# Transformer block on one core: the context projected a batch ahead, self-attention's values ahead of its transposes, and cross-attention's V padded with zeros

## The reference

```python
h = layernorm(x, ln1_g, ln1_b)
x = attention(h, h, a1_Wq, a1_Wk, a1_Wv, a1_Wo, a1_bo) + x        # self
h = layernorm(x, ln2_g, ln2_b)
x = attention(h, context, a2_Wq, a2_Wk, a2_Wv, a2_Wo, a2_bo) + x  # cross
h = layernorm(x, ln3_g, ln3_b)
u, gate = split(h @ ff_Wp + ff_bp)
return (u * gelu(gate)) @ ff_Wo + ff_bo + x
```

## Time and profile before

| | |
|---|---|
| median of 3 runs | 1007.19 us (997.95 to 1015.29) |
| the profiled execution | 1004.74 us |
| span in its trace | 1002.9 us |
| mean granted clock of TensorE | 0.966 of full speed |
| PE busy in the span | 931.9 us (93%) |
| DVE | 768.2 us (77%) |
| ACT | 672.5 us (67%) |
| POOL | 388.3 us (39%) |

### The profile page before, as it was taken

How to read it: one execution, slowest core, us unless ns; L and a number is a source line. 1 busy time by engine, 2 the same in 40 slices (tenths; PEclk the granted TensorE clock), 3 DMA queues, 4 the chain that set the end, 5 groups by cost and what they waited for, 6 DMA issues and landing times.

```text
span 1002.9 us, 21207 instructions
## 1 busy us (share of the span) xinstructions
PE 931.9 (93%) x7252; PEld 864.4 (86%) x7252; DVE 768.2 (77%) x1658; ACT 672.5 (67%) x2009; POOL 388.3 (39%) x498
## 2 busy tenths in 40 slices
PE   7799998899999999999997899899899897899998
PEld 6687877798989899999987798898898896799998
DVE  5576678979888988888897887886787877566674
ACT  5556556878786877777787678776677777343333
POOL 1211445534443444434333545544545555201010
PEclk9799999999999999999999899997899998899999
DMA  7311101224111111111142134212212212100100
GB/s 222 97 50 42 37 22 36 56 47 103 25 47 23 49 34 33 34 38 44 23 106 49 45 73 104 56 28 54 55 29 54 52 33 80 37 33 32 33 23 22
DMA packets 85745, 51.67 MB, mean 52 GB/s; under 512 B 43272, under 2 KB 79112, under 8 KB 85640
## 3 DMA queue, kind: packets, MB, share of 16 engines
q1 hardware_dynamic: 85640, 50.32, 19.3%
HBM read 41.64 MB, written 8.65 MB: 50 GB/s over the span
## 4 chain that ended last, share of the span: by engine, by line
PE 70%; DVE 13%; ACT 9%; issue 4%; DMA 2%; POOL 1%; SPq 1%; DVEq 0%; POOLq 0%
PE bank L1444 10%; PE bank L1445 9%; PE bank L1446 9%; PE bank L1461 5%; PE bank L1704 5%; PE bank L1684 5%; PE bank L1733 4%; PE bank L1734 4%; ACT p L809 3%; PE bank L1752 3%; PE bank L1754 3%; PE bank L1753 3%; PE bank L1713 1%; PE bank L1566 1%; PE bank L1567 1%
## 5 line engine op out<-in xcount | busy, mean ns | idle before, releaser
L613 POOL TENSOR_TENSOR oT_scaled<-oT,rsumT 128x256 f32<-128x256 f32 x128 | 98.2, 767 | 318.6 <-DVE oT L1239 177.4
L809 ACT ACTIVATE p<-bank,negmax 128x256 f32<-128x256 f32 (+1 forms) x512 | 207.6, 427 | 18.5 <-DVE negmax L1202 12.5
L1444 PE MATMUL bank<-hT_hi,w_hi 128*128 128x256 f32 x640 | 190.2, 297 | 8.5 <-DVE qkT_lo L1271 2.9
L1445 PE MATMUL bank<-hT_lo,w_hi 128*128 128x256 f32 x640 | 180.4, 282 | 0.0
L1446 PE MATMUL bank<-hT_hi,w_lo 128*128 128x256 f32 x640 | 180.3, 282 | 0.0
L1444 PEld LDWEIGHTS bank<-hT_hi,w_hi 128*128 128x128 f32 x640 | 123.3, 193 | 13.1 <-issue 10.2
L1445 PEld LDWEIGHTS bank<-hT_lo,w_hi 128*128 128x128 f32 x640 | 122.8, 192 | 0.0
L1446 PEld LDWEIGHTS bank<-hT_hi,w_lo 128*128 128x128 f32 x640 | 122.4, 191 | 0.0
L1733 PE MATMUL bank<-pT_hi,v_hi_lo 128*128 128x256 f32 (+1 forms) x384 | 102.2, 294 | 14.8 <-DVE oT L1239 4.9
L819 ACT CAST pT_hi<-bank 128x512 fp32r<-128x512 f32 x128 | 68.9, 591 | 67.6 <-PE bank L1704 67.5
L809 ACT ACTIVATION_READ_ACCUMULATOR p<-bank,negmax 128x1 f32 x512 | 110.0, 215 | 0.0
(11 more groups left out here) (204 smaller groups left out, 2788.8 us busy)
## 6 DMA issues: line engine op xcount, KB each, us to landing
rsumT<-rsums_dram SPq DMA_DIRECT2D x256, 64.0 KB, 2.8
w_stage<-in_weights SPq DMA_DIRECT2D x47, 256.0 KB, 4.5
x_in<-x_dram SPq DMA_DIRECT2D x24, 256.0 KB, 3.6
x_dram<-x_out SPq DMA_DIRECT2D x16, 256.0 KB, 3.3
l_x<-in_x SPq DMA_DIRECT2D x4, 512.0 KB, 5.2
x_dram<-l_out SPq DMA_DIRECT2D x4, 512.0 KB, 2.8
rsums_dram<-rsum SPq DMA_DIRECT2D x128, 2.0 KB, 3.2
out_dram<-x_out SPq DMA_DIRECT2D x8, 256.0 KB, 2.1
```

What stands on the lines that cost most here:

```text
L613: nc.gpsimd.tensor_tensor(on[:, :].rearrange("p (t q) -> p t q", t=NT), of[:, G % DEEP, :].rearrange("p (t q) -> p t q", t=NT), rT[:, G % ...
L809: last = nc.scalar.activation(p[:, G % 2, e, t * cols:(t + 1) * cols], scores_at(G, e, t), ACT.Exp, bias=negmax[:, G % 2, t, e:e + 1], acc ...
L1444: nc.tensor.matmul(dst, lh, rh, start=(i == 0), stop=False)
L1445: nc.tensor.matmul(dst, lh, rl, start=False, stop=False)
```

## The change

Three parts, in two kinds of step.

*The context a batch ahead.* A second pair of buffers holds cT_hi and cT_lo (`c_hi(b)`, `c_lo(b)`, by the parity of b; the room is taken from a buffer that served as filler). Transposes, rounding and low half of a cross batch's context move from steps i=3 and 4 of the batch before it to the last step (i=7) of the batch before that, and into bank 3. `project_keys(b+1, 0)` stays at i=4 and takes over the wait for `h_full`. DVE's `prepare_lo` of a cross batch moves from i=3 to i=4.

*One order.* In a self step `weighted_values(G-1)` now follows `scores(G+1)` at once, as in a cross step; ACT's `copy_low_values(G-1)` and DVE's `add_low_values(G-1)` move up ahead of `round_pT` and `pT_low` in theirs.

*Cross-attention's V.* V is laid out as head, 64 zeros, head for each pair, high halves in one plane and low halves in another. Six matmuls of 256 columns, where there were four, gather a pair's outputs in one half of a bank: high by high and high by low of the probabilities, and low by high, for each of the two heads. Nothing is copied or added: DVE's `normalise_o(G-2)` multiplies the bank by rT into `oT`, and POOL's `split_o` has two operations, two steps behind. POOL sets V's zeros, and those of the keys that DVE set before.

```diff
+            ch2 = sb("cT_hi2", [128, KT, SC], F32R, where=l1)
+            cl2 = sb("cT_lo2", [128, SC], F32R, where=l1)
@@ banks
-            return bank[4 if b == B else 7]
+            return bank[4 if b == B else 3]
@@ POOL step
+                if b == B - 1 and i == 4:
+                    zero_keys(0, G)
+                if b == B and i == 0:
+                    zero_keys(1, G)
+                if b == B - 1 and i == 5:
+                    zero_values(0, G - 1)
+                if b == B and i == 1:
+                    zero_values(1, G - 1)
...
-                if G >= 1:
+                if 1 <= G <= STEPS // 2:
                     split_o(G - 1)
+                if G >= STEPS // 2 + 2:
+                    split_o(G - 2)
@@ ACT step_self
+                if G >= 1:
+                    copy_low_values(G - 1)
                 round_pT(G)
                 softmax_pair(G + 1)
...
-                if G >= 1:
-                    copy_low_values(G - 1)
+                if turn and i == 7:
+                    round_context(B + 1)
@@ ACT step_cross
-                if i == 4 and more:
-                    round_context(b + 1)
...
-                copy_low_values(G - 1)
+                if G == STEPS // 2:
+                    copy_low_values(G - 1)
...
+                if i == 7 and b + 2 < 2 * B:
+                    round_context(b + 2)
@@ DVE
+            def normalise_o(G):
+                dve.wait_ge(y["o"], G + 1)
+                dve.wait_ge(*spread_until(G))
+                dve.wait_ge(y["o_norm" if G - DEEP < STEPS // 2 else "o_lo"], G - DEEP + 1)
+                nc.vector.tensor_tensor(of[:, G % DEEP, :].rearrange("p (t q) -> p t q", t=NT),
+                                        o_bank(G).rearrange("p (t q) -> p t q", t=NT),
+                                        rT[:, G % DEEP, :].rearrange("p (q t) -> p t q", t=NT),
+                                        ALU.mult).then_inc(y["o_sum"], 1)
@@ DVE step_self
+                if G >= 1:
+                    add_low_values(G - 1)
                 pT_low(G)
...
-                if turn and i == 4:
-                    zero_keys(0, G)
-                if G >= 1:
-                    add_low_values(G - 1)
@@ DVE step_cross
-                if i == 4 and more:
-                    context_low(b + 1)
...
-                add_low_values(G - 1)
+                if G == STEPS // 2:
+                    add_low_values(G - 1)
+                if G >= STEPS // 2 + 2:
+                    normalise_o(G - 2)
                 pT_low(G)
...
-                if i == 3:
+                if i == 4:
                     prepare_lo(b + 1)
...
+                if i == 7 and b + 2 < 2 * B:
+                    context_low(b + 2)
@@ PE
             def context(b):
                 pe.wait_ge(y["c_in"], 32 * (b - B + 1))
+                if b > B:
+                    pe.wait_ge(y["qk_lo"], query_product(b - 1, 1))
@@ PE weighted_values
+                if b >= B:
...
+                    for e in range(2):
+                        vc = slice(g * 3 * DH + e * DH, g * 3 * DH + e * DH + 128)
...
@@ PE step_self
                 scores(G + 1)
+                if G >= 1:
+                    weighted_values(G - 1)
                 transpose_p(G)
...
-                if G >= 1:
-                    weighted_values(G - 1)
@@ PE step_cross
-                if i == 3 and more:
+                if i == 4 and more:
                     pe.wait_ge(y["h_full"], KT * (b + 2))
-                    context(b + 1)
-                if i == 4 and more:
                     project_keys(b + 1, 0)
+                if i == 7 and b + 2 < 2 * B:
+                    context(b + 2)
```

More of the change, by code:

```diff
@@ L344, in v_src, with padded @@
             return v_bank(b, c)[0:v_rows(b), :].rearrange("p (g e d) -> p g e d", g=4, e=2)
+        def padded(c):
+            return vv[0:SC, :, 0:PAIRS * 3 * DH].rearrange("p j (g s d) -> p j g s d", g=PAIRS, s=3)[:, :, 4 * c:4 * c + 4, :, :]
         def v_dst(b, c, low):
+            if b >= B:
+                return padded(c)[:, int(low), :, 0:3:2, :]
             part = vv[0:v_rows(b), c // 2, c % 2 * 4 * 2 * VW:(c % 2 + 1) * 4 * 2 * VW]
@@ L391, in o_bank @@
         def o_bank(G):
-            return bank[6 if G < STEPS // 2 or G % 2 else 2]
+            return bank[6] if G < STEPS // 2 else bank[6 if G % 2 else 2][:, 0:S]
         def pT_both(G):
@@ L619, in split_o, with zero_values @@
+                nc.gpsimd.tensor_tensor(oh[:, G % PAIRS, :], full, ones[:, :], ALU.mult).then_inc(y["o_hi"], 1)
                 pool.wait_ge(y["o_hi"], G + 1)
-                nc.gpsimd.tensor_tensor(ol[:, G % PAIRS, :], on[:, :], oh[:, G % PAIRS, :].bitcast(F32),
+                nc.gpsimd.tensor_tensor(ol[:, G % PAIRS, :], full, oh[:, G % PAIRS, :].bitcast(F32),
                                         ALU.subtract).then_inc(y["o_lo"], 1)
+            def zero_values(c, read):
+                pool.wait_ge(y["o"], read)
+                pool.wait_ge(y["o_lo"], read - 1)
+                nc.gpsimd.memset(padded(c)[:, :, :, 1, :].bitcast(F32), 0.0).then_inc(v_zeros_ready, 1)
+                pool.wait_ge(v_zeros_ready, c + 1)
@@ new lines, in zero_keys @@
+            def zero_keys(c, read):
+                pool.wait_ge(y["scores"], read)
+                pool.wait_ge(y["o_lo"], read - 1)
+                for n, k_ in enumerate((kdh, kdl)):
+                    nc.gpsimd.memset(k_[0:DH, 4 * c:4 * c + 4, SC:2 * SC].bitcast(F32), 0.0).then_inc(zeros_step, 1)
+                    pool.wait_ge(zeros_step, 4 * c + 2 * n + 1)
+                    nc.gpsimd.memset(k_[DH:128, 4 * c:4 * c + 4, 0:SC].bitcast(F32), 0.0).then_inc(zeros_step, 1)
+                    pool.wait_ge(zeros_step, 4 * c + 2 * n + 2)
+                pool.sem_inc(zeros_ready, 1)
@@ L800, in round_context @@
                 act.wait_ge(y["cT"], b - B + 1)
[L801 removed]
+                nc.scalar.copy(c_hi(b)[:, :, :], c_src(b)).then_inc(y["cT_hi"], 1)
             def softmax_pair(G):
@@ L1320, in step_self @@
                     weights_lo(dve, 10 + i)
-                if turn and i == 4:
-                    zero_keys(0, G)
-                if G >= 1:
-                    add_low_values(G - 1)
+                if turn and i == 7:
+                    context_low(B + 1)
             def step_cross(G):
@@ L1388, in feed_forward @@
                         f_low(it, j - 1)
+                    if it == 0 and j == 0:
+                        normalise_o(STEPS - 2)
                     if it == 0 and j == 1:
-                        add_low_values(STEPS - 1)
                         weights_lo(dve, 25)
+                    if it == 0 and j == 2:
+                        normalise_o(STEPS - 1)
                     if it == 0 and j == 3:
@@ L1803, in project_values @@
                 else:
-                    last = context_product(dst, w, (ch[:, 0, :], cl[:, :], ch[:, 1, :]), False)
+                    last = context_product(dst, w, (c_hi(b)[:, 0, :], c_lo(b)[:, :], c_hi(b)[:, 1, :]), False)
                 last.then_inc(y["v"], 1)
             def project_keys(b, c):
-                pe.wait_ge(y["cT_lo"], b - B + 1)
+                pe.wait_ge(y["cT_lo"], b - B + (2 if c == 1 and b + 1 < 2 * B else 1))
                 if c == 1 or b == B:
@@ L1868, in step_self @@
                     project_out(b, 0, 3)
+                if turn and i == 7:
+                    context(B + 1)
             def step_cross(G):
```

54 lines of the change are left out of this document (31 added, 23 removed).

## The result

| | before | after |
|---|---|---|
| median of 20 runs each, us | 1008.77 | 1018.02 |
| span of the profiled execution | 1002.9 | 1012.3 |
| matmuls of PE | 7252 | 7380 |

The ratio is 1.0104, with a 95% interval of 1.0083 to 1.0125: the change costs one per cent. That is a small sum of large terms of both signs. The two spans differ by 9.4 us. Cut at the starts of the scores, they differ by +28.0 us in the self stage with the turn (380.7 to 408.7), −18.3 from there to the first scores of the last cross batch (268.9 to 250.6), −0.6 behind those (193.2 to 192.6) and +0.2 ahead of all.

A forecast was written before the change was run, and what follows sets the result against it. PE was taken to bound the self stage, with cross-attention looser, mostly at i=4 and 5. 1004.7 + 15.4 − 27 − 3 − 2 + 19 + 13 = 1020.1, forecast 1020 us; 8 in 10: 994 to 1041.

The forecast's parts named there:

- padded V: Cross-attention: 128 more weighted_values matmuls at 0.12 us each, with nothing on PE to cover them, +15.4 us.
- context ahead: Cross steps i=4 and 5: the 12.7 us wait and three quarters of the slow matmuls go, −27 us.
- wait for V: Self step i=5: PE idles 2.35 us for V's low half in each of eight batches, +19 us.
- clock's echo: Self batches: clock falls after that wait, 1.6 us a batch as middle of two rows, +13, bounds 0 and 26.
- turn: Between self and cross stages: POOL zeroes keys instead of DVE, shortening PE's waits, −3 us, bounds 0 and −4.25.
- end: Kernel's end: a shorter chain cuts PE's 4.4 us of waits for oT_lo, −2 us, bounds 0 and −4.4.
- The estimate of 1033: Whole kernel: time if the skill page's clock cycling puts the echo nearer its upper end, 1033 us.
- I take 0, bounds 0 and −4: Cross stage: relief of DVE, ACT and POOL by padded V gains 0, since neither DVE nor ACT sets the end.
- the self stage keeps its clock: Rival, self stage: the wait is there but no clock fall follows, 1007 us; chance 0.18.
- the context stays on the path: Rival, cross stage: wait moves to another operand, only 10 of the 27 us come back, 1037 us; chance 0.06.
- DVE's wait for the spread sums: Rival, cross steps: normalise_o waits for the rT transfer, late in the odd case only; +21, 1041 us; chance 0.08.
- the sign that I gave: Cross stage: no wait of DVE for rT of over a microsecond.

The follow-up runs named there:

- context alone: The kernel before with only the context a batch ahead (and prepare_lo at i=4): 979.01 us, ratio 0.9748 to the kernel before.
- self order undone: The changed kernel with the self step's order of before on PE, ACT and DVE: 987.41 us, ratio 0.9831 to the kernel before.
- stall filled: The changed kernel with 20 matmuls before the wait for V's low half, step i=5 of self batches 0 to 6: 1008.68 us, ratio 1.0044.
- the run with V first: The changed kernel with DVE making V's low half before the row maxima in self step i=5: 999.99 us, ratio 0.9958.
- the run with the self order alone: The kernel before with only the self step's new order added: 1035.47 us, ratio 1.0308.

## Why the prediction was right, point by point

The time (1020 against 1018.02) and its sign were right, and the mechanism that carried it, PE's wait for V's low half, was there eight times, at 2.3 us in seven of them and 4.3 in the first. Term by term:

| term | forecast | measured | from |
|---|---|---|---|
| padded V | +15.4 | +8.4 | context alone and self order undone |
| context ahead | −27 | −25 | context alone, spans 1002.9 and 977.8 |
| wait for V | +19 | +17.7 | waits: 20.5 after, 2.8 before |
| clock's echo | +13 | +7 | stall filled: 7.3 us in six batches |
| wait for l_out, first batch | not in the sum | +3.2 | the changed kernel's trace |
| turn | −3 | about −2 | by its named waits; not separated |
| end | −2 | −0.6 | spans behind the last batch's first scores; not separated |

That the sum of these came within 2 us of the time is in part luck: the padding was put 7 us too high and the echo 6, and against them stand the smaller gains of context, turn and end and what the first batch costs, which was not in the sum.

*The wait* was the term read best: 2.35 us from two rows of before, 2.32 found. But eight times 2.35 takes all batches for equal. The first and the last already waited, 1.49 and 1.27 us, and the first now waits 4.3, and 3.2 more for l_out; it grew by 7.5 us where the sum had 4.

*The echo* was mis-sized: 1.6 us a batch, 1.2 measured, with four batches at 0.97 and two of six at 1.00 (five and one in the second profiled execution of the same kernel). The step that failed was taking the middle of two rows: a batch pays 1.7 us or nothing. Its cause was right, as the filled stall shows. Nothing in the traces told which of the batches would show it. The trace bears out the Trainium skill's "TensorE: Matmul & The Clock Gate", section "A second HAM failure mode: psum-queue depth-cycling", in kind; that section gives no size. The clock does go back and forth with short idle times, at 1.7 us in a batch that shows it and 4.0 in batch 7 of the filled kernel, and the 1.15 us wait of the run with V first left it at 1.00. The estimate of 1033 that I derived from it was 15 us too high.

*The padding* failed at "nothing covers the two more" and at "I take 0, bounds 0 and −4" for DVE's relief. Both took the steps of before, where i=3 holds the context's transposes and is 3.73 us long. Once the context has gone, i=3 is 3.32, DVE with prepare_full in its queue is late at i=4, and two adds less are worth 0.35 us there. I costed two edits of one change each against the kernel before, not against each other. The 0.12 us a matmul is right for steps where PE is the bound (0.23 for two).

*The context* gave nearly what was forecast, though not as I summed it. The two steps take 9.2 us, not 8.03, and 0.92 of the difference is that wait for DVE at i=4; all of the slow clock came back, not three quarters of it. The seven windows gave 23.1 us (91.1 to 68.0), and most of the rest is that i=3, rid of the transposes, is 0.4 us shorter in each batch, of which i=7, which now has them, takes back 0.2.

*Turn and end* stay open. Between the first scores of batch 7 and those of batch 9 the kernels have 99.3 us before, 93.8 after, 95.4 with the self order undone and 97.0 with the context alone. The changed kernel in its second profiled execution has 95.6, so one execution differs from the next by as much as the term, and batch 8's steps i=4 and 5, which belong to the context, are in all of them. Of the named waits, the 2.87 us for the low half of the queries became 2.04. Behind the first scores of the last cross batch there are 193.2 us before and 192.6 after, and 193.7 in the run with the self order alone, whose code there is that of before. The end gave 0.6 us of the 2, and no run tells even that from chance; PE waits there for oT, 2.75, 2.11 and 3.18 us, by the changed kernel's trace.

*The rivals.* That the self stage keeps its clock came true in two of six batches, that the context stays on the path in none. DVE's wait for the spread sums, which I had put at the odd case, is there. In the changed kernel DVE stands idle ahead of normalise_o for 12.4 us in 16 waits (L1297), three of them over a microsecond, against the sign that I gave. The longest:

```profile
710.33 0.42 DVE L1297 TENSOR_TENSOR oT<-bank,rsumT 128x256 f32<-128x256 f32 x1 [2.15 <-issue]
```

The profile names no releaser, but the transfer that it needs was issued at 706.10 and landed 4.1 us later, at 710.2. The low half of the probabilities comes behind it, PE waits 1.02 us for that at 711.45, and this step, i=6 of batch 11, took 5.82 us in place of 4.58. With the self order undone the longest is 2.50 us, and its step, i=6 of batch 9, took 6.22. So the mechanism was real and its price a few microseconds at most, not 21, in the profiled executions. Another sign was off as well: PE does wait for the low half of the probabilities in cross steps, 0.33 us at i=4 in batches 10 to 14.

## What to carry to other kernels

When a consumer is moved earlier in an in-order queue, look up for every operand, step by step, when it is done and what now stands between; an order that is right in seven steps of eight cost more here than the rest of the change gained. Cost two edits of one change against each other: taking work out of one step made another engine late there, and so changed what the second edit was worth. When a wait only moves as one engine's work is shuffled, look whether that engine is really full: here DVE stood idle for 1.17 us, behind ACT, which waited for the very operation that had been moved.

## What was unexpected

An idle time of 2.3 us in the equal batches, whose matmuls are otherwise unbroken, cost 1.7 us more in clock or nothing (0.97 over a batch of 50.7 us), one of 1.15 us nothing, and twenty matmuls of no use in its place were free and kept the clock: the kernel with 20 x 7 more matmuls has a ratio of 1.0044, the one without 1.0104 and 1.0082 (the intervals overlap for the second). The kernel with two more matmuls in each cross step took 4666.8 us in one of its eight runs, with the same instructions, DVE as busy as ever (732 us), the granted clock at 1.00 and a matmul of L1501 at 888 ns on the mean against 283; no run here tells why.
